# Norm scalars moved from VectorE to GpSimd, norm tiles split 1:3, scatters in halves, and new instruction orders on four engines

## The reference, cut to what matters

```python
x = x + causal_attention(layernorm(x), ctx, ctx)         # per sequence of 64 tokens
n = layernorm(x)                                         # second norm
logits = n @ gate_w.T                                    # 8 experts
_, idx = top_k(logits + beta, 2)
c = zeros.at[idx].add(sigmoid(logits[idx]))
routed = sum_e c[e] * (silu(n @ gate[e]) * (n @ up[e])) @ down[e]     # hidden size 256
shared = (silu(n @ sg) * (n @ su)) @ sd
x = x + routed + shared
```

## Time and profile before

| | us |
|---|---|
| median of 3 runs | 396.43 (396.29 to 396.60) |
| profiled execution, its own time | 396.57 |
| its span on the core | 394.9 |
| PE busy | 379.7 (96%) |
| DVE busy | 294.4 (75%) |
| ACT busy | 236.2 (60%) |
| POOL busy | 251.0 (64%) |

### The profile page before, as it was taken

How to read it: one execution, slowest core, us unless ns; L and a number is a source line. 1 busy time by engine, 2 the same in 40 slices (tenths; PEclk the granted TensorE clock), 3 DMA queues, 4 the chain that set the end, 5 groups by cost and what they waited for, 6 DMA issues and landing times.

```text
span 394.9 us, 11090 instructions
## 1 busy us (share of the span) xinstructions
PE 379.7 (96%) x3321; PEld 318.3 (81%) x3321; DVE 294.4 (75%) x1308; ACT 236.2 (60%) x558; POOL 251.0 (64%) x275
## 2 busy tenths in 40 slices
PE   8979999999999999899999999999999999999993
PEld 3445666666666665689999999999999999999993
DVE  4988989999998896687966666667677666666662
ACT  2689898798888863355566565652211565656540
POOL 6636888888877787338787788886100045645464
PEclk9999999999999999999999999999999999999998
DMA  7953464896442112247556775554332113332223
GB/s 239 354 165 103 141 210 136 253 280 199 136 149 83 64 62 77 70 120 143 104 86 91 87 100 77 72 81 59 59 74 55 36 21 54 45 48 23 26 22 27
DMA packets 43049, 41.78 MB, mean 106 GB/s; under 512 B 5688, under 2 KB 31808, under 8 KB 42992
## 3 DMA queue, kind: packets, MB, share of 16 engines
q1 hardware_dynamic: 30864, 30.69, 26.8%
q0 software_dynamic: 12128, 10.40, 19.1%
HBM read 24.17 MB, written 16.90 MB: 104 GB/s over the span
## 4 chain that ended last, share of the span: by engine, by line
PE 57%; POOL 1%; issue 1%; DVE 1%; ACT 0%; POOLq 0%; DVEq 0%
PE gu_pair L1609 35%; PE bank L1633 17%; PE bank L1575 2%; PE bank L1548 1%; POOL out L529 1%; PE bank L1536 0%; PE gu_pair L1822 0%; POOL sorted_rows L478 0%; PE bank L1527 0%; DVE acc L1008 0%; PE gu_pair L1560 0%; DVE hid L1002 0%; ACT tile_T L727 0%; DVE t_out L1211 0%; DVE t_part L1205 0%
## 5 line engine op out<-in xcount | busy, mean ns | idle before, releaser
L529 POOL DMA_INDIRECT out<-t_out,tile_in x64 | 100.2, 1565 | 85.0 <-DVE t_out L1211 70.6
L1609 PE MATMUL gu_pair<-tile_T,W_slot 128*128 128x128 f32 x1024 | 124.8, 275 | 0.5 <-ACT tile_T L727 0.5
L1609 PEld LDWEIGHTS gu_pair<-tile_T,W_slot 128*128 128x128 f32 x1024 | 119.5, 192 | 0.7 <-issue 0.7
L756 ACT ACTIVATE t_silu<-gu_pair 128x512 f32<-128x512 f32 (+1 forms) x78 | 46.4, 594 | 101.8 <-PE gu_pair L1609 94.8
L1171 DVE SCALAR_TENSOR_TENSOR t_hid<-t_silu,gu_pair 128x512 f32<-128x512 f32 (+1 forms) x78 | 53.1, 680 | 48.4 <-PE gu_pair L1609 47.2
L1633 PE MATMUL bank<-W_down,t_hid 128*128 (+1 forms) x620 | 82.3, 276 | 0.1
L478 POOL DMA_INDIRECT sorted_rows<-rows,slot x64 | 63.4, 990 | 20.5 <-issue 20.0
L1633 PEld LDWEIGHTS bank<-W_down,t_hid 128*128 128x128 f32 x620 | 75.4, 192 | 0.7 <-issue 0.7
L746 ACT ACTIVATE W_slot<-W 128x512 f32 x128 | 73.2, 622 | 3.9 <-DVE slot_pair L1062 2.0
L489 POOL DMA_INDIRECT left_in<-sorted_rows,left_index x27 | 26.1, 967 | 16.8 <-DVE left_index L1089 8.9
L441 POOL TENSOR_TENSOR rstd<-var_eps,minus_half 128x8 f32<-128x8 f32 (+1 forms) x19 | 27.9, 1470 | 10.9 <-DVE var_eps L902 10.5
(11 more groups left out here) (158 smaller groups left out, 543.5 us busy)
## 6 DMA issues: line engine op xcount, KB each, us to landing
tile_in<-sorted_rows SPq DMA_DIRECT2D x91, 66.5 KB, 2.0
x_sb<-x SPq DMA_DIRECT2D x16, 256.0 KB, 4.4
c_T<-ctx_cols SPq DMA_DIRECT2D x16, 256.0 KB, 3.1
c_sb<-ctx SPq DMA_DIRECT2D x16, 256.0 KB, 4.6
out<-acc SPq DMA_DIRECT2D x16, 256.0 KB
sorted_rows<-padding SPq DMA_DIRECT2D x1, 2128.0 KB, 12.7
sorted_rows<-left_in SPq DMA_DIRECT2D x27, 66.5 KB, 2.4
sorted_rows<-rows,slot POOLq DMA_INDIRECT x64, 3.1
```

Source lines behind the costliest of these rows:

```text
L529: e.indirect_dma_start(out_flat, bass.IndirectOffsetOnAxis(ap=tile_in[:, tiles_of(i)[0] % NR, ID:ID + 1].bitcast(I32), axis=0), t_out[:, q ...
L756: e.activation(t_silu[:, 0:n * M], gate_up_pair[i % 2][0][:, 0:n * M], ACT.Silu).then_inc(s_t_silu, 1)
L1609: r = e.matmul(bank[:, c:c + P], w, tile_T[:, i % TX, tile], start=True, stop=True, skip_group_check=True)
```

## The change

- DVE loses `variances` and `shifts`. POOL gets them: `variances` as two instructions (minus mean, variance plus epsilon), `shifts` as one product.
- `normalise_x` on POOL does one tile instead of two, `shift_x` on ACT three instead of two, from group 4 on.
- `scatter(g)` becomes `scatter(g, 0)` and `scatter(g, 1)` with two indirect DMAs each, placed separately.
- The picks of groups 13, 14 and 15 go from POOL to DVE (`pick_late`).
- SP issues x of group 1 and the router before ctx of group 0, and x of groups 2 and 3 before ctx of groups 1 and 2.
- The padding constants on POOL come behind `variances(1)`.
- The lists of calls of POOL, ACT, DVE and PE are reordered throughout. PE has four `keep_warm` matmuls more, all before `route(0)`.

```diff
@@ sync_program
             load_x(0)
-            load_c(0)
             load_x(1)
             e.dma_start(router[:], gate_w).then_inc(s_router_in, 16)
+            load_c(0)
+            load_x(2)
             load_c(1)
-            load_x(2)
+            load_x(3)
             e.dma_start(beta_all[:], ...
             load_c(2)
-            load_x(3)
@@ gpsimd_program
+            def variances(j):
+                n = norms(j)
+                if j < G:
+                    e.wait_ge(s_moments[0], j + 1)
+                if j >= LEAD:
+                    e.wait_ge(s_moments[1], j - LEAD + 1)
+                if j:
+                    e.wait_ge(s_shift, j)
+                    e.wait_ge(s_rstd, j)
+                e.tensor_scalar(minus_mean[:, n], moments[:, j % 2, n, :, 0], -1.0, None, ALU.mult).then_inc(s_minus_mean, 1)
+                e.tensor_scalar(var_eps[:, n], moments[:, j % 2, n, :, 1], EPS, None, ALU.add).then_inc(s_var_eps, 1)
+            def shifts(j):
+                n = norms(j)
+                e.wait_ge(s_minus_mean, j + 1)
+                e.wait_ge(s_rstd, j + 1)
+                e.tensor_tensor(shift[:, j % 2, n], minus_mean[:, n], rstd[:, j % 2, n], ALU.mult).then_inc(s_shift, 1)
             def normalise_x(g):
                 e.wait_ge(s_rstd, g + 1)
-                for i in range(GT // 2):
-                    r = e.tensor_scalar(xn[:, i], ...
+                e.tensor_scalar(xn[:, 0], ...
-            def scatter(g):
+            def scatter(g, half):
...
-                for i in range(GT):
+                for i in range(half * GT // 2, (half + 1) * GT // 2):
@@ scalar_program, shift_x
-                for i in range(GT // 2, GT):
+                for i in range(GT // 2 if g < FIRST else 1, GT):
@@ vector_program
-            def variances(j): ...
-            def shifts(j): ...
+            def pick_late(g):
+                e.wait_ge(s_is_chosen, g + 1)
+                e.wait_ge(s_tanh, g + 1)
+                e.wait_ge(s_weights, g)
+                e.tensor_tensor(picked[:, :, :, 0:E], is_chosen[:, :, :, :], ...
@@ vector_program, the list from row_max(2) on (new)
             row_max(2)
             normalise_first(3)
             statistics(5, 0)
             inverse_sums(2)
             bias_logits(0)
             choose(0)
             slots(0)
             weights(0)
             row_max(3)
             residual(2)
             statistics(2, 1)
             bias_logits(1)
             choose(1)
...
@@ gpsimd_program, the end of the list (new)
             variances(17)
             powers(17)
             shifts(17)
             scatter(12, 1)
             scatter(13, 0)
             variances(18)
             powers(18)
             shifts(18)
             scatter(13, 1)
             scatter(14, 0)
             scatter(14, 1)
             scatter(15, 0)
             scatter(15, 1)
@@ tensor_program, from score(2) on (new)
             score(2)
             keep_warm(4)
             transpose_xn2(0)
             keep_warm(3)
             route(0)
             shared_gate_mm(0, 0)
             turn_logits(0)
             transpose_probs(2)
             transpose_xn(3)
             shared_gate_mm(0, 1)
             transpose_xn2(1)
             ranks(0)
             mask_scores(3)
             score(3)
             attend(2)
             route(1)
             shared_up_mm(0, 0)
             turn_logits(1)
             transpose_xn(4)
             transpose_probs(3)
             shared_up_mm(0, 1)
             ranks(1)
             shared_gate_mm(1, 1)
@@ tensor_program, the end of the list (new)
             ranks(15)
             shared_up_mm(14, 1)
             list_ends()
             shared_down_mm(13)
             shared_up_mm(15, 0)
             shared_gate_mm(15, 0)
             shared_gate_mm(15, 1)
             spread_table()
             shared_down_mm(14)
             shared_up_mm(15, 1)
             shared_down_mm(15)
```

More of the change, by code:

```diff
@@ L581, in gpsimd_program @@
+            shifts(7)
             token_numbers(3)
             token_numbers(4)
[L583 to L599, removed]
+            for g in range(2, 6, 2):
+                scatter(g, 1)
+                pick(g + 1)
@@ L1272, in vector_program @@
             choose(2)
+            sum_up(0)
+            statistics(7, 0)
+            slots(2)
+            hidden(1, 1)
             hidden(1, 0)
[L1274 to L1275 removed]
+            weights(2)
+            row_max(5)
             inverse_sums(4)
[L1277 to L1279 removed]
             residual(4)
[L1281 to L1289 removed]
+            statistics(4, 1)
@@ new lines, in vector_program @@
+            statistics(8, 0)
+            bias_logits(3)
+            inverse_sums(5)
+            choose(3)
+            sum_up(1)
+            hidden(2, 1)
+            slots(3)
+            hidden(2, 0)
+            weights(3)
+            row_max(6)
+            residual(5)
+            statistics(5, 1)
+            hidden(3, 0)
+            bias_logits(4)
+            choose(4)
+            statistics(9, 0)
+            hidden(3, 1)
+            weights(4)
+            for g in range(2, 6, 2):
@@ L1311, in vector_program @@
+                hidden(g + 3, 0)
+                weights(g + 4)
+                hidden(g + 3, 1)
+            slots(8)
+            inverse_sums(10)
+            sum_up(6)
+            row_max(11)
+            residual(10)
             statistics(10, 1)
-            statistics(13, 0)
-            variances(13)
+            statistics(14, 0)
             bias_logits(9)
+            sum_up(7)
             choose(9)
-            shifts(13)
-            hidden(8, 0)
-            slots(9)
             inverse_sums(11)
@@ L1700, in tensor_program @@
+            attend(4)
+            route(3)
+            shared_gate_mm(2, 0)
+            shared_up_mm(2, 0)
+            transpose_xn(6)
+            turn_logits(3)
+            shared_down_mm(1)
+            transpose_probs(5)
+            shared_up_mm(2, 1)
+            mask_scores(6)
+            shared_gate_mm(3, 1)
+            ranks(3)
+            transpose_xn2(4)
+            score(6)
+            attend(5)
+            shared_gate_mm(3, 0)
+            for g in range(2, 6, 2):
                 route(g + 2)
@@ L1720, in tensor_program @@
-                transpose_probs(g + 5)
-                ranks(g + 3)
-                shared_up_mm(g + 2, 0)
+                mask_scores(g + 6)
+                attend(g + 5)
+                transpose_xn2(g + 4)
+                shared_gate_mm(g + 3, 0)
+                score(g + 6)
+            route(8)
+            shared_up_mm(7, 0)
+            shared_up_mm(7, 1)
+            turn_logits(8)
+            shared_down_mm(6)
+            shared_gate_mm(8, 1)
+            transpose_xn(11)
+            transpose_probs(10)
```

543 lines of the change are left out of this document (303 added, 240 removed).

## The result

| | us | ratio to before, 95% interval |
|---|---|---|
| before, median of the runs beside it | 396.51 (396.29 to 396.92) | |
| after | 412.47 (411.66 to 413.36) | 1.0402 [1.0377, 1.0427] |
| after, profiled execution and its span | 413.36; 411.6 | |

What follows compares the result with a forecast made beforehand. PE was taken to pace stage 1: 37.15 (start 2.9 us late) + 127.7 of work + 2.65 of waits = 167.5 against 167.34, so 396.6 us, set at 396.4. The 8-in-10 range was 393.6 to 399.0.

Steps and rivals of the forecast that it cites:

- Stage 2 is untouched: After stage 1: the change can only move stage 2's start, 169.98 us; the handover from the last down stays 2.64 us.
- PE paces stage 1 of before: Stage 1 after 34 us: PE's work is 127.9 of 133.1 us, so lighter DVE and POOL win back at most 5.2.
- The stall of statistics(5, 0): DVE, ahead of bias_logits(0): waits over 3 us for x of group 5 until 26.5; shared_gate_mm(1, 1) starts 2.9 us late.
- a backlog: DMA engines, full until 26 us: x of group 5 comes last and lands at 26.5 whatever the x order.
- The waits behind it: PE from shared_gate_mm(1, 1) to the last down: 2.65 us of waits, possibly 1.3 to 5.2, against 5.2 before.
- The small instructions on POOL: Three scalar instructions per norm round on POOL at 0.17 us each: plus 0.5, net -0.3 with one 0.79 tile gone.
- The slower rival: Stall paid and waits stay, if POOL's small instructions cost over 0.26 us each: 397.9 to 399.2 us, chance 0.26.
- Half scatters: POOL: the same 64 DMAs, no extra cost; a norm's scalars pass after two scatters instead of four, 2.6 us sooner.
- the third tile on ACT: ACT: at most 0.48 us more per group, taken for nothing since ACT is busy 101 of 133 us.
- picks on DVE: Late groups: three instructions of about 0.22 us on DVE, ending PE's 0.63 us wait for a hidden product.
- The last wait, 0.88: PE before the last down: stays near 0.85 us, as hidden(15, 1) must stand between its up and its down.
- The port: SBUF port shared by DVE and POOL: mutual waits could cost 3.6 us, giving 400 us; chance 0.03.

Runs made afterwards that it cites:

- b_tiles13: The kernel before with one norm tile on POOL and three on ACT from group 4 on; 396.21 us, ratio 0.9989.
- b_early_x: The kernel before with statistics of x one group earlier from group 8 on and x loads issued ahead of the ctx loads; 395.91 us, ratio 0.9989.
- b_best: The kernel before with earlier statistics, x loads ahead of ctx, one norm tile less on POOL, and picks 13 to 15 on DVE; 395.68 us, ratio 0.9971.
- a_x_ahead: The changed kernel with each x load in SP's loop issued ahead of the ctx loads; 404.87 us, ratio 1.0206.
- a_s5: The changed kernel with statistics(5, 0) back behind choose(0), nothing else; 409.13 us, ratio 1.0286.
- a_x_s5: The changed kernel with x loads ahead of ctx and statistics(5, 0) behind choose(0), scalars left on POOL; 401.71 us, ratio 1.0111.
- a_x_dve: The changed kernel with x loads ahead of ctx and variances and shifts back on DVE; 403.87 us, ratio 1.0177.
- a_x_dve_s5: The changed kernel with x loads ahead of ctx, variances and shifts back on DVE, and statistics(5, 0) behind choose(0); 400.01 us, ratio 1.0087.
- a_lead3_dve: The changed kernel with statistics(j, 0) from 8 on behind statistics(j - 3, 1) again, and variances and shifts back on DVE; 408.09 us, ratio 1.0291.
- a_lead3: The changed kernel with statistics(j, 0) from 8 on behind statistics(j - 3, 1) again, nothing else; 412.29 us, ratio 1.0388.
- a_dve: The changed kernel with variances and shifts back on DVE, nothing else; 420.72 us, ratio 1.0581.
- b_stats_early: The kernel before with statistics of x one group earlier on DVE from group 8 on; 422.30 us, ratio 1.0642.
- b_scalars_pool: The kernel before with variances and shifts moved from DVE to POOL; 411.04 us, ratio 1.0364.

## Why the prediction was wrong

**Stage 2 is untouched, PE paces stage 1 of before.** Right: 224.9 us follow in both, and b_tiles13, b_early_x and b_best show that air on POOL and DVE and earlier x are worth 0 to 0.3%.

**The stall of statistics(5, 0).** Right to two tenths:

```profile
26.56 0.87 DVE L984 BATCH_NORM_STATS2 stats<-x_sb 128x6 f32<-128x128 f32 x4 [4.17 <-DMA x_sb<-x]
...
31.23 0.42 DVE L1010 TENSOR_REDUCE neg_max<-gu_pair 128x4 f32<-128x256 f32 x1
```

```profile
35.60 1.12 PE L1637 MATMUL bank<-xn_T,shared_gu 128*128 128x512 f32 x2 [1.41 <-ACT silu_g L798]
...
36.99 1.04 PE L1628 MATMUL bank<-xn_T,shared_gu 128*128 128x512 f32 x2
```

The prediction had 26.5, 31.4, 35.75 and 37.15 for these four. That this load is held by a backlog also holds: issued ahead of ctx in a_x_ahead, it still lets DVE go only at 25.86 (the DMA engines were not full until 26 us, though, as the prediction says; their share was 0.68). The price of 2.9 us was right where it was put: shared_gate_mm(1, 1) comes 3.1, 2.8 and 2.7 us later with the early call than with the late one (after and a_s5, a_x_ahead and a_x_s5, a_x_dve and a_x_dve_s5). The whole time moves by more, 3.6 to 4.6. A part of that is likely the clock, which the prediction had nowhere: PE is busy for only 5.3 to 6.6 of the 10 us from 20 to 30 in the six traces of the changed kernel and its variants with the early call, and in four of them the granted clock falls in the next 10 us, to 0.83 (a_x_ahead), 0.75 (a_lead3_dve) and 0.69 (a_lead3, a_dve); in the three traces with the late call, where PE is busy for 8.4 to 9.1, it stays at 1.00. In a_x_dve the one execution at a mean clock of 0.998, the profiled one, took 402.4 us, 2.9 more than the profiled one of a_x_dve_s5, and the three at 0.989 and 0.990 took 403.8 to 404.2.

**The waits behind it. This is the step that failed.** The sum put them at 2.65 us, 5.2 at most. The last down starts at 182.23:

```profile
182.23 2.02 PE L1649 MATMUL bank<-shared_dn,hid 128*128 128x128 f32 x16 [0.88 <-DVE hid L1106]
```

182.23 + 1.79 - 36.99 - 127.7 = 19.3 us of waits, where the prediction had 2.65. The trace names 15.2 of them, in 18 waits of PE, and at most 1.7 are the clock; in before it names 2.3, in four. The question "is x there when DVE comes?" was put to group 5 and to no other. But the diff moves `statistics(j, 0)` for every j from 8 on from behind `statistics(j - 3, 1)` to behind `statistics(j - 4, 1)`, while `load_x(j)` stays behind `load_c(j)` on SP and that behind `attend(j - 4)`. The trace of before had all that was needed: the order of SP, and the waits of DVE for x, of which there are two, 2.38 at the very first statistics and 1.21 at `statistics(5, 0)`, and none behind, because the statistics came a group later. In after, 10.8 of the 18.1 us lie behind `statistics(5, 0)`. Taking that cause away alone gives back 7 to 8 of the 16 us (a_x_ahead), and applying it alone to before costs 6.4%. By the same sum the waits are 10.4 us in a_x_ahead (last down at 173.03, shared_gate_mm(1, 1) at 36.74). So late x is 8.9 of the 19.3. In a_x_dve_s5, with late x, the scalars on POOL and the early `statistics(5, 0)` all taken back, they are still 8.8 us, over the 5.2 that the prediction allowed at most: the rest of the new lists adds waits rather than ending them. The range failed with it, since its upper end assumed that the waits could at worst stay.

**The small instructions on POOL.** Mis-sized. The prediction took 0.17 us each, +0.5 a round, from the nearest rows of another engine. Busy they are 0.24 to 0.26 and 0.20, but from start to start 0.33, and with the wait of the shift behind the power 0.99 us a round. With two tiles left on POOL this costs 3.6%; with one, as in the change, 1.4% in the old order and 0.2 to 0.3% in the new one, where x is early. The slower rival named the mechanism and a bound of 0.26 us each that lay in the right place, but added only 2.6 us for it. And it set the scalars against the norm tile that leaves, round for round: the last rounds have no such tile, and there the scalars are paid in full.

**Half scatters, the third tile on ACT, picks on DVE.** The third tile is hidden, as costed (b_tiles13). The down of group 14 had no wait (178.48 in after), and no norm tile of POOL is waited for late in stage 1; PE waits for one once, 0.64 us at 46.72. The last wait, 0.88, stayed to the hundredth, and the handover of 2.64 too. The half scatters are not quite free on POOL: its 64 scatters take 64.6 us against 63.4, and the issue before them 22.4 against 20.0. No run takes the halves or the picks of the changed kernel back alone, so what they are worth there is not shown.

**The port.** Hardly a stretch of POOL's or DVE's instructions is to be seen in after: the 12 tiles of L465 took 805 ns on average, against 791 before, and `is_chosen` 218 against 219. A cost of 3.6 us from this is not in the trace.

## What to carry to other kernels

When a list is reordered, go through every step that consumes a load and compare its new place with the moment of issue, which is bound by whatever stands ahead of it on the queue of loads; one group checked is not all. An operation that moves to another engine must be priced from start to start on that engine, with what it does to the gap before the next entry, and in the rounds that have nothing to give in exchange. And a bound on waits taken from the old order is no bound for a new one: here, with PE, DVE and POOL all over 85% busy in the middle of the stage, one late input stopped all three.

## What the runs showed of the hardware

A product of 128x8 on POOL takes 0.25 us and a new one starts every 0.33; the power of 128x4 took 1.04 us and of 128x8 1.67; an estimate from these two sizes is 0.16 per column and 0.4 that does not shrink. An x load of 256 KB issued at 51.92 released DVE at 56.76, 4.8 us later; the DMA engines were 72% busy between the two. The granted clock fell once in stage 1 of after:

```profile
110.00:120.00 10.00, 8.23 (x68) 5.29 (x68) 7.34 (x44) 7.30 (x22) 6.74 (x11) 1.00 0.39 129
120.00:130.00 10.00, 10.00 (x82) 6.64 (x81) 6.32 (x37) 7.80 (x23) 5.96 (x10) 0.83 0.44 131
```

0.83 is a mean of the two levels, 2.4 and 1.2 GHz: it was 0.50, which is 1.2 GHz, from about 120 to 123.5, behind a stretch in which PE was busy for 8.23 of 10 us; in before it was 1.00 in every window of 10 us of stage 1. At most 1.7 us of the 19.3 (10 times 0.17) are this. Other runs pay more, at most 8.5 us in b_stats_early and 11.9 in a_dve, and those without late x and without the early `statistics(5, 0)` pay nothing (1.00 in every such window of b_scalars_pool, b_best, a_x_s5 and a_x_dve_s5). So waits of PE can cost a second time, by the clock. They need not: in after itself PE was busy for only 5.73 of the 10 us from 20 to 30, and the clock stayed at 1.00.
